# One ring of seven PSUM banks in place of rings of three, two and two

## What is computed

```
x = x + 0.5 * _L0_ffn_ref(_layernorm(x, axis=-1), ...)
x = x + _L0_attn_ref(_layernorm(x, axis=-1), ...)
x = x + 0.5 * _L0_ffn_ref(_layernorm(x, axis=-1), ...)
x = x + 0.5 * _L1_ffn_ref(_layernorm(x, axis=-1), ...)
x = x + _L1_attn_ref(_layernorm(x, axis=-1), ...)
x = x + 0.5 * _L1_ffn_ref(_layernorm(x, axis=-1), ...)
```

```
dots = jnp.einsum('bhnd,bhmd->bhnm', q, k) * scale
attn = jax.nn.softmax(dots, axis=-1)
out = jnp.einsum('bhnm,bhmd->bhnd', attn, v)
```

## Time and profile before

| what | value |
|---|---|
| median of 3 runs | 3542.43 us (3540.39 to 3547.53) |
| the profiled execution: its time | 3528.64 us |
| the profiled execution: its span | 3526.8 us |
| PE busy | 3064.0 us, 87% |
| DVE busy | 2162.2 us, 61% |
| POOL busy | 1744.9 us, 49% |
| ACT busy | 1727.9 us, 49% |

### The profile page before, as it was taken

The page is one execution under the profiler, slowest core; times in us unless marked ns, Lnnn a source line. Parts: engine busy times, 40 slices in busy tenths (PEclk is TensorE's granted clock), DMA queues, the critical chain, the costliest instruction groups (busy, mean ns, idle before and its releaser), DMA issues.

```text
span 3526.8 us, 46628 instructions
## 1 busy us (share of the span) xinstructions
PE 3064.0 (87%) x16106; PEld 1908.2 (54%) x16106; DVE 2162.2 (61%) x4520; ACT 1727.9 (49%) x3306; POOL 1744.9 (49%) x1540
## 2 busy tenths in 40 slices
PE   7999999999999999888845749999999999998266
PEld 6884455454545545477734735545545455554166
DVE  5567666767666676556665326666666656666542
ACT  5565666666676666656622314343444434343022
POOL 0006887878787787821003714443444444444046
PEclk9999999999999999999967969999999999999578
DMA  2003333333333333200012344343434434333024
GB/s 87 1 19 91 91 73 91 82 83 91 73 91 76 88 90 75 55 31 17 16 31 51 63 104 102 85 90 87 100 79 96 91 79 90 90 85 73 24 67 74
DMA packets 182987, 254.00 MB, mean 72 GB/s; under 512 B 35904, under 2 KB 75584, under 8 KB 182208
## 3 DMA queue, kind: packets, MB, share of 16 engines
q1 hardware_dynamic: 168672, 240.19, 28.8%
q0 software_dynamic: 14080, 10.82, 2.3%
HBM read 33.44 MB, written 16.67 MB: 14 GB/s over the span
## 4 chain that ended last, share of the span: by engine, by line
PE 58%; DVE 10%; DMA 9%; POOL 9%; SPq 6%; ACT 4%; issue 4%; another core or an unknown queue 0%; POOLq 0%; ACTq 0%; DVEq 0%
PE psum L778 20%; PE psum L808 9%; DMA stack<-halves 7%; PE psum L745 6%; PE psum L766 6%; SPq L1827 5%; POOL arena L1735 5%; PE psum L678 5%; PE psum L862 3%; PE psum L838 2%; PE psum L770 2%; PE psum L683 2%; POOL sums L1768 2%; ACT arena L1117 1%; DVE halves L1349 1%
## 5 line engine op out<-in xcount | busy, mean ns | idle before, releaser
L1735 POOL TENSOR_TENSOR arena<-arena 128x512 f32<-128x512 f32 x1152 | 1439.4, 1277 | 921.1 <-ACT arena L1117 897.8
L778 PE MATMUL psum<-stack 96*128 96x512 f32 (+4 forms) x4096 | 1356.1, 445 | 107.7 <-DMA stack<-halves 79.7
L1373 DVE TENSOR_REDUCE top<-psum 128x1 f32<-128x512 f32 x1536 | 1002.7, 686 | 456.4 <-PE psum L778 452.3
L778 PEld LDWEIGHTS psum<-stack 96*128 96x128 f32 (+4 forms) x4096 | 711.7, 192 | 723.0 <-issue 364.2
L1117 ACT ACTIVATE arena<-psum 128x512 f32<-128x512 f32 x1536 | 866.7, 595 | 449.6 <-PE psum L778 438.3
L808 PE MATMUL psum<-arena,values 128*32 128x512 f32 (+1 forms) x3072 | 559.5, 617 | 0.0
L1704 POOL TENSOR_SCALAR rstd<-mv 128x4 f32<-128x4 f32 x56 | 12.7, 226 | 582.3 <-DVE mv L1239 580.6
L766 PE MATMUL psum<-xT,wqkv 128*128 128x512 f32 x512 | 272.5, 614 | 5.9 <-DVE recips L1397 2.8
L1080 ACT ACTIVATE halves<-psum,bqk 128x512 fp32r<-128x512 f32 x128 | 88.0, 687 | 362.0 <-PE psum L766 362.0
L1405 DVE RECIPROCAL psum<-psum 128x128 f32<-128x128 f32 x256 | 226.4, 926 | 61.6 <-PE psum L838 61.6
L1325 DVE SCALAR_TENSOR_TENSOR X<-psum,weight,X 128x128 f32<-128x128 f32 x512 | 144.0, 344 | 142.6 <-PE psum L745 142.5
(11 more groups left out here) (154 smaller groups left out, 3067.4 us busy)
## 6 DMA issues: line engine op xcount, KB each, us to landing
stack<-halves SPq DMA_DIRECT2D x768, 128.0 KB, 2.3
stack<-halves SPq DMA_DIRECT2D x384, 256.0 KB, 4.8
tokens<-xn SPq DMA_DIRECT2D x16, 256.0 KB, 2.4
sums<-X SPq DMA_DIRECT2D x16, 256.0 KB, 3.8
wqkv<-in_wg SPq DMA_DIRECT2D x16, 256.0 KB
wqkv<-in_wu SPq DMA_DIRECT2D x16, 256.0 KB
wqkv<-in_wd SPq DMA_DIRECT2D x16, 256.0 KB
wqkv<-in_w_qkv SPq DMA_DIRECT2D x2, 1536.0 KB, 9.8
```

The lines of the kernel that those rows point to most:

```text
L778: ins = T_.matmul(bk, st[0:k, side, slot + h, cols], st[0:k, 1 - side, slot + h, :], start=r == 0, stop=r == len(PARTS[l]) - 1)
L1373: give(V_.reduce_max(top[i][:, j:j + 1], psum[:, bank[key], :], AX.X), key)
L1735: ins = G_.tensor_tensor(to[:, h, :], old[:, h, :], prob[l][tile % N_PROB][:, h, :], ALU.add)
```

## The change

All uses but the mixed values take their bank from one ring of seven. No instruction is added, taken away or moved on any engine; line numbers go down by one. What differs is which bank each fill has, and so which former use its wait names.

```
     def __init__(self, order):
-        self.scores, self.probs = Ring((0, 1, 5)), Ring((2, 3))
-        self.mixed, self.other = Ring((4,)), Ring((6, 7))
+        self.banks, self.mixed = Ring((0, 1, 2, 3, 5, 6, 7)), Ring((4,))
...
     def compute0(self, s, b):
         def up(e):
             for c in range(2):
-                self.once(self.scores, ("up", s, b, e, c))
+                self.once(self.banks, ("up", s, b, e, c))
...
     def project(self, l, n):
         for w in "qkv":
-            self.once(self.other, (w, l, n))
+            self.once(self.banks, (w, l, n))
...
     def maxima(self, l, n):
         for i in range(HEADS[l] * TILES_B):
-            self.once(self.scores, ("score", l, n, i))
+            self.once(self.banks, ("score", l, n, i))
             yield
...
             for h in range(HEADS[l]):
-                self.once(self.probs, ("prob", l, n, kt, h))
+                self.once(self.banks, ("prob", l, n, kt, h))
                 yield
...
     def mix(self, l, n):
         dn, turned, back = ("dn", l, n), ("turned", l, n), ("back", l, n)
-        self.other.take(dn)
+        self.banks.take(dn)
         yield
         if l == 0:
-            self.other.give(dn)
+            self.banks.give(dn)
             yield
-            self.other.take(turned)
+            self.banks.take(turned)
             yield
-            self.other.give(turned)
+            self.banks.give(turned)
             yield
-            self.other.take(back)
+            self.banks.take(back)
             yield
-            self.other.give(back)
+            self.banks.give(back)
             yield
         else:
             for _ in range(TILES_B):
                 yield
-            self.other.give(dn)
+            self.banks.give(dn)
             yield
```

More of the change, by code:

```diff
@@ L181, in __init__ @@
         play(order, parts)
-        rings = (self.scores, self.probs, self.mixed, self.other)
+        rings = (self.banks, self.mixed)
         self.bank = {k: p for r in rings for k, p in r.at.items()}
@@ L201, in normalise @@
         yield
-        self.once(self.other, ("norm", key))
+        self.once(self.banks, ("norm", key))
         self.xn.give(key)
@@ L208, in scored @@
         yield
-        self.once(self.other, ("logit", key))
+        self.once(self.banks, ("logit", key))
         self.xt.give(key)
@@ L235, in compute0 @@
                 yield
-            self.once(self.probs, ("down", s, b, e))
+            self.once(self.banks, ("down", s, b, e))
             yield
@@ L247, in maxima @@
         for i in range(HEADS[l] * TILES_B):
-            self.once(self.scores, ("score", l, n, i))
+            self.once(self.banks, ("score", l, n, i))
             yield
     def rows(self, l, n):
-        self.once(self.other, ("top", l, n))
+        self.once(self.banks, ("top", l, n))
         yield
@@ L287, in mix @@
                 yield
-            self.other.give(dn)
+            self.banks.give(dn)
             yield
     def out(self, l, b):
-        self.other.take(("out", l, b))
+        self.banks.take(("out", l, b))
         for _ in range(8):
             yield
-        self.other.give(("out", l, b))
+        self.banks.give(("out", l, b))
         yield
@@ L303, in settle @@
         self.moments.give(("y", b))
-        self.other.take(("settle", b))
+        self.banks.take(("settle", b))
         yield
-        self.other.give(("settle", b))
+        self.banks.give(("settle", b))
         yield
     def fold(self):
-        self.once(self.other, ("fold",))
+        self.once(self.banks, ("fold",))
         yield
     def experts1(self, s):
-        self.once(self.other, ("weights", s))
+        self.once(self.banks, ("weights", s))
         for bit in range(TOP_BIT, -1, -1):
[L316 to L320, removed]
+            self.once(self.banks, ("reach", s, bit))
+        self.once(self.banks, ("threshold", s))
+        self.once(self.banks, ("inside", s))
+        self.once(self.banks, ("totals", s))
+        self.once(self.banks, ("tokens", s))
         def turn(e):
             for part in range(2):
-                self.once(self.other, ("rows", s, e, part))
+                self.once(self.banks, ("rows", s, e, part))
         turn(0)
@@ L329, in experts1 @@
                 for half in range(2):
-                    self.once(self.scores, ("gate", s, e, f, half))
-                    self.once(self.probs, ("wide", s, e, f, half))
+                    self.once(self.banks, ("gate", s, e, f, half))
+                    self.once(self.banks, ("wide", s, e, f, half))
             if e + 1 < EXPERTS:
@@ L334, in experts1 @@
             self.once(self.mixed, ("narrow", s, e, 0))
-            self.once(self.probs, ("narrow", s, e, 1))
+            self.once(self.banks, ("narrow", s, e, 1))
         yield
```

## The result

| kernel | median us | runs, lowest to highest |
|---|---|---|
| before | 3541.41 | 4 runs, 3539.74 to 3547.53 |
| changed | 3593.32 | 4 runs, 3590.24 to 3598.82 |

The ratio is 1.0145, with a 95% interval of 1.0126 to 1.0164: 52 us slower. In a later comparison, beside the experiments e7 to e9, the ratio was 1.0159 (1.0145 to 1.0173). The forecast was 3610 us, with a range of 3568 to 3642. The traced execution of the change has a span of 3594.4 us against 3526.8, so the two traces differ by 67.6 us, more than the medians; I come back to that.

The account below looks back on a forecast made before the run. PE, busy 87% of the span, was taken as the bound; terms 78 - 28 - 14 + 15 + 22 - 1 gave +72, taken as +68 us on 3542.4: 3610 us, 1.9% slower, range 3568 to 3642.

Parts of the forecast that it names:

- likeliest case: The forecast itself: the waits of Parts 1 and 5 are paid in full, 3587 to 3637 us; chance 0.68.
- Part 1: Layer 0: k waits for DVE to free back's bank, 1.30 us in 60 groups, +78 us.
- Part 2: Layer 0: PE's waits for two probability banks go, 0.5 us in 56 groups, -28 us.
- Part 3: Layer 0: other bank waits, such as back for q and q for turned, go, 1.8 us a batch, -14 us.
- Part 4: Layer 0: a score waits for out's bank (+7 us) and a probability for settle's (+8 us), once a batch.
- Part 5: Layer 1: a score waits for dn's bank, less the logits' own bank wait, which goes; +22 us.
- the rest: Expert stages: waits for a reader shrink by 3 us, one wait on the last out adds 2; -1 us.
- Half absorbed: Rival: PE's pause at k empties other engines' queues and shortens later waits; +39 for +78, about 3571 us; chance 0.16.
- Faster: Rival: the rotation wins because DVE frees the banks before PE arrives; about 3500 us; chance 0.06.
- Worse: Rival: k's DMAs miss the next scores, or layer 0's granted clock falls to 0.95; 3670 us; chance 0.07.

Follow-up runs that it names:

- e7: e4 with POOL's second and third additions cut to the first half of the columns, leaving sums incomplete: 0.9713 of before.
- e9: e4, except that settle keeps its place in the ring as in the change: 0.9947 of before.
- e1: Kernel before with its old rings, plus one wait in layer 0: k of group n waits for back of group n-4: 1.0203 of before.
- e4: The change's ring of seven, but a bank goes to the end of the ring when given back, not when taken: 0.9874 of before.
- e6: The change, but all fills except back go to the end of the ring when given back: 1.0018 of before.
- e3: Kernel before, but scores and probabilities (and up, down, gate, wide) share a ring of five; slow users keep two banks: 0.9967 of before.
- e5: The change, but back alone goes to the end of the ring when given back: 1.0061 of before.
- e2: Kernel before with its old rings, plus one wait in layer 1: the second score of group n waits for dn of group n-3: 1.0059 of before.
- e10: The kernel before, unchanged, run again for a second trace: 1.0002 of before.

## Why the prediction was right

The kind, the place and the sign were right; the median was 17 us under the forecast, inside the likeliest case's own range. The traced execution of the change took 3596.17 us where the prediction has 3597. The 17 us are the step from there to the median: I put the change's median 13.8 us above its trace, as before's was, and it lies 2.9 below. Point by point:

- **Part 1, `k` behind `back`, +78 us.** Right. 60 waits, 1.87 us from the scores to `k` as forecast, handover 0.05 us. By itself it lengthens layer 0 by 75.8 us (e1) and the program by 72. My upper bound and my reason, that nothing hides it, hold for the old rings; behind e4's ring POOL hides a part (50 us, e6).
- **Part 2, two probability banks, -28 us.** Right in the change: ten products in 2.45 us as forecast, and the ordinary group is 0.71 us shorter than with the wait at `k` alone (19.10 to 18.39). But it is a gain only while something else slows PE. Alone (e3) it is worth 0.15 us a group. PE's step from the matmul ahead of `dn` to `dn`, which waits for POOL's sums, is 0.33 us in an ordinary group before, 0.53 in e3, 0.9 in e4 and 0.32 in e7. So POOL takes 0.2 of the 0.35 us that are missing in e3; the other 0.15 are open.
- **Part 3, other bank waits, -14 us.** About right: the six places other than 2 and 3 together are 5.8 us shorter in the change than in e1, where parts 2 and 3 would give 42 / 8 = 5.3 for the whole batch.
- **Part 4, `out` and `settle`, +15 us.** Under-sized; this is the term that was most wrong. The waits were sized about right: `out` costs 0.97 us at place 2 (e4 to e5) where I had 0.86, and the pause for `settle` is 2.64 us where I had 1.58 and 0.95 on top, 2.53. What I put at nothing, without a reason, is the clock after that pause. Against e6, which lacks the waits for `settle` and `out`, place 3 of the change is 3.0 us longer. Against the batches of before without a half clock it grew from 19.2 to 22.8, by 3.6 us: 1.30 for `k`, 0.95 for `settle`, and 1.3 for 3.4 us at half clock, by the price read from before itself. Before the change this came in 3 or 4 of 7 batches, after it in all, and in 2 of them for 6.8 us (23.9 and 24.0 us). Place 2 grew by 2.28 us, where `k` and `out` take 2.4: the gain of part 2 is only 0.1 us there (24.26 to 24.15 in e4), not 0.5. I had read a granted clock of 1.00 for layer 0, a mean of 450 us rounded to two figures, which has one stretch of 3.4 us at half clock in it.
- **Part 5, layer 1, +22 us.** The mechanism was right (54 waits, as counted from the plan), and the loss as well: 26 us in e2. The gain against it was under-sized: the trace of before shows 0.8 us of idle time for the logits' bank, but the step from `top` to the logits is 1.08 us before and 0.11 after in seven batches, so -7 us and not -4. And here the change took half clocks away: at place 3 of layer 1 before has one in 4 of 7 batches (3 of 7 in e10), with 19.8 to 20.4 us instead of 18.84, and the change has none in either trace (18.35 us). That is some -5 us, which I had not counted. Together, 26 - 7 - 5 = 14; layer 1 grew by 12.4 and 8.8 us in the two pairs of traces. I take the remaining difference to lie in groups that wait for DMA and differ from one execution to the next; this is not shown.
- **The sum.** Layer 0: 78 - 28 - 14 + 15 = 51 forecast, 58 in the traces; layer 1: 22 and about 10; the rest -1 and about -3. The traces differ by 67.6 us where I forecast 68; the medians by 52. That the traces come so near is in part luck: layer 0 grew by 7 us more than forecast and layer 1 by about 12 less.

**The rivals.** *Half absorbed* had its 3571 outside the result, and yet there is something in it: in a ring without the other slow users, the wait at `k` costs 50 us and not 78, as POOL would hold PE anyway. *Faster* in the form forecast, with the order of the change, did not come, but it is what the ring would have done with another rule for the held banks: 0.9874. The Trainium skill (Perfetto Trace Analysis, Matmuls) says that independent groups should rotate through different banks so that evacuation overlaps the next products. Here the runs agree for scores and probabilities alone (five banks in the order in which they were taken, 0.33% faster, e3). With the slow users in the same ring they agree only when the rotation goes by the time a bank is given back: seven banks in the order in which they were taken are 1.45% slower than three fixed rings, and in the order in which they were given back 1.26% faster. (The advice to use all eight banks stands on that page under Matmul Optimizations, not where the prediction puts it; all eight are in use in both kernels.) *Worse* by missed DMAs did not come: over the whole span PE's waits for the DMA of `stack` are 81.4 us in 46, where they were 79.7 in 46. Its other half, a lower granted clock in layer 0, came in small: 0.984 on average where before has 0.993.

## What to carry to other kernels

Before pooling PSUM banks, go through the users whose reader is late because of its place in an in-order queue, and for each ask which fill is sent to its bank next, and whether the reader itself waits for something that PE issues just ahead of that fill; such a pair cost its whole round trip here (1.30 us in 60 groups), with seven banks in the ring. Separate rings were not waste here: they kept slow users out of the main stream. If banks are pooled, order them by when they come free and not by when they were taken; and look at what stands second in line (here POOL's sums), since it decides how much a removed wait is worth. Last, read the granted clock behind each long pause of TensorE group by group, not as a mean: here a pause of 2.6 us had a second cost behind it, about as large as what the change had added to the pause.

## What the runs showed that I had not expected

- The cost of one wait depends on the waits around it, by a factor that matters: the wait for `back` was worth 76 us, 52 us or 44 us in layer 0 of the traces (e1 over before, e6 over e4, the change over e5), and 72, 50 or 30 by the ratios.
- Once a batch, one bank that is given to the wrong user costs PE 3 us, 26 us in all by the ratios and 30 in layer 0 (e9). About half of that is the longer pause, the other half 3.4 us at half clock behind it.
- Sixty idles of 1.14 us in layer 0 left the granted clock alone (e1 and e6 have no half clock from batch 1 on). Pauses of 1.4 to 1.7 us were followed by 3.4 us at half clock in some groups and not in others, and those of 2.6 us in every batch.
- POOL is busy 49% of the span and still sets the pace of an ordinary group of layer 0 as soon as the bank waits are gone: 17.5 us a group with its sums, 16.96 with a part of them left out. The share of the whole span hides this: in layer 0 it is busy 360 of 450 us.
